# Two composed weights in the setup of a gated recurrent layer, made ahead of the inp product, and the order of the first loads and steps

## The chip, the cores and the metric

The kernel runs on one core of one Trainium2 chip. The metric is the time of one execution on the device in microseconds (us); the changed kernel is compared with this one by the median of their runs. The engines are TensorE (PE), VectorE (DVE), ScalarE (ACT), GpSimd (POOL) and SyncE (SP), which here only issues DMAs. Each runs its own queue of instructions in order and waits on semaphores.

## The reference

x and the context are (32, 128, 256) float32: 32 sequences of 128 steps. For each step, with k = v = context and q = the normalised x:

```
r = decay * r + k * v;  retained = q * r
inp = retained @ Wi.T + bi
gate = sigmoid(inp @ Wg.T + bg)
state = tanh((gate * state + (1 - gate) * inp) @ A.T + inp @ Bm.T)
out = state @ Wo.T + bo
```

Then x = x + tanh(g) * out, a layer norm, and a feed-forward layer: a shared SwiGLU part plus the two best of 8 experts with their softmax weights; it is added to x with a factor tanh(g_ffn).

## The kernel before

The 128 steps are cut into 16 tiles of 8 steps; a tile is 256 tokens (8 steps by 32 sequences). Tile by tile the kernel normalises x, turns the context, squares it, scans it (r), multiplies (ret), splits ret in a high and a low half, and makes three products of ret: inp, gate, and the Bm addend. gate and Bm need products of weights, Wi with Wg and Wi with Bm ("composed" weights), made once in the setup. A recurrence step (L602, L607) adds A times the blended state to the bank rec; ScalarE takes the tanh (`tanh_step`, L1004), and VectorE blends state and gate for the next step (`gated_state`, L1315 u_hi, L1317 u_full, L1320 u_lo). The step that works on tile i also carries parts of tiles i+1, i+2 and of the feed-forward layer of i-1, i-2 between its 8 steps. All these places are written out by hand, one list for each engine; the semaphores setup_pe, setup_dve and setup_act count the setup's results, so each wait names a position in another engine's list.

The setup is one straight list on each engine ahead of the loop, with tile 0's work and its 8 steps in it. `square` loads a 256 x 256 weight, `load_x` and `load_c` load a tile of x (one DMA) and of the context (four DMAs with rows of 32 numbers). On TensorE: WARMUP = 6 products of the identity with itself (L731), Wi, Wg and Bm transposed (L554), tile 0's x transposed (L668), the composed Wg (L562) into bank rec[1], the inp product (L577), 16 small products for the biases (L749), the gate product, A transposed, the composed Bm (L562) into rec[1] again, tile 1's x transposed, Wo transposed (L763), the addends with Bm and with A (L719), and step 0. ScalarE copies each result out of its bank (L1113 to L1131) and squares the context (L1015); VectorE makes the low halves (L1275). Behind step 5 stand the column norms of the weights sh and w1 (L788), whose maxima VectorE takes (L1568), and the scales of the feed-forward weights; ScalarE scales and casts sh and w1 in these steps, and GpSimd makes their low halves (L1840, sh_lo and w_lo).

Of the kernel before, what the change touches and what calls it, by code (L numbers as in the profile page):

```python
# [44 lines left out]
P = 128  # L45
B, S, D = 32, 128, 256
KC = D // P
# [57 lines left out]
def gated_layer(nc, x, ctx_in, g_xattn, g_ffn, Wi, bi, Wg, bg, A, Bm, Wo, bo, decay,  # L105
                w_shared_in, w_shared_out, w1_shared, w2, w_gate, gate_bias, out):
    with ExitStack() as stack:
# [323 lines left out]
        def _(sp):  # L431
# [13 lines left out]
            def square(n, w):  # L445
                sp.dma_start(raw_sq[n][:, :, :], w.rearrange("(k p) i -> p k i", p=P)).then_inc(load[n], 16)

            load_x(0, first)
            square("Wi", Wi)
            square("Wg", Wg)  # L450
            load_c(0, first)
            with nc.allow_non_contiguous_dma(reason="small vectors"):
                square("Bm", Bm)
                load_x(1, first)
                square("A", A)
# [93 lines left out]
        def _(pe):  # L549
# [179 lines left out]
            for n in range(WARMUP):  # L729
                at = slice((n * P) % (KC * TOK), (n * P) % (KC * TOK) + P)  # L730
                pe.matmul(flat(rec[0][:, :, :])[:, at], ident[:, :], ident[:, :], start=(n == 0),  # L731
                          stop=(n == WARMUP - 1), skip_group_check=True)
            pe.wait_ge(load["Wi"], 16)
            transposed(bank[3], raw_sq["Wi"]).then_inc(setup_pe, 1)
            pe.wait_ge(load["Wg"], 16)
# [3 lines left out]
            x_transposed(0, first)  # L739
            pe.wait_ge(setup_act, 3)  # L740
            composed(flat(rec[1][:, :, :]), WgT).then_inc(setup_pe, 1)
            pe.wait_ge(setup_dve, 2)
            inp_product(0, first)
            pe.wait_ge(load["biases"], BIASES)
            pe.wait_ge(setup_act, 4)
# [11 lines left out]
            composed(flat(rec[1][:, :, :]), BmT).then_inc(setup_pe, 1)  # L757
            x_transposed(1, first)
            pe.wait_ge(load["Wo"], 16)
            pe.wait_ge(setup_dve, 6)  # L760
# [5 lines left out]
            pe.wait_ge(setup_act, 6)  # L766
            pe.wait_ge(setup_dve, 7)
            addend_bm(0, first)
            addend_a(0, first)
            pe.wait_ge(setup_dve, 8)  # L770
            recurrence(0, 0, first)
            inp_product(1, first)
            recurrence(0, 1, first)
            gate_product(1, first)
            recurrence(0, 2, first)
# [8 lines left out]
            pe.wait_ge(scale_chain, 1)  # L784
            pe.wait_ge(squares_ready, 2)
            for n, at in (("sh", bank[0]), ("w1", bank[5])):
# [3 lines left out]
                last.then_inc(wsum_done, 1)  # L790
            recurrence(0, 6, first)
            recurrence(0, 7, first)
# [205 lines left out]
        def _(act):  # L998
# [20 lines left out]
            def bias_set(a, k):  # L1019
# [3 lines left out]
                if k.static and a == 0:  # L1023
                    act.wait_ge(setup_dve, 6)
# [86 lines left out]
            context_squares(0, first)  # L1111
# [3 lines left out]
            act.copy(flat(WgT[:, :, :]), bank[4][:, :]).then_inc(setup_act, 1)  # L1115
            act.wait_ge(setup_pe, 3)
# [886 lines left out]
```

## Time and profile before

| | us |
|---|---|
| median of 3 runs (lowest, highest) | 480.12 (478.55, 481.08) |
| the profiled execution's own time | 479.74 |
| its span | 478.0 |
| TensorE busy in the span | 424.7 |
| VectorE busy | 359.7 |
| ScalarE busy | 224.3 |
| GpSimd busy | 194.4 |

A timeline row has the start in us from the span's start, the time in us it covers, the engine (PEld is TensorE's weight load, SPq the issuing queue), the line, operation, what it writes <- reads, and how many instructions; in brackets how long the engine idled before it and what ended that. A float32 product shows as two matmuls in the rows of the same count. "Granted clock" is the clock of TensorE as a share of its full 2.4 GHz; the lower level is 1.2 GHz.

### The profile page before, as it was taken

The numbers are of one execution on the slowest core, as the hardware profiler recorded it, in microseconds if no ns is written. First come the engines' busy times: TensorE is split into PE (matmuls) and PEld (weight loads), VectorE is DVE, ScalarE is ACT, GpSimd is POOL, SyncE is SP. The second block draws the span as 40 slices with busy tenths as digits, with TensorE's granted clock in tenths as the row PEclk, the third lists the DMA queues.
The fourth block names the chain that finished last, engine by engine and source line by source line (L and its number), as shares of the span: only waits on it lengthen the run. The fifth ranks groups of instructions, "written<-read, shape, count | busy, mean of one in ns | idle before, by whom it ended". The sixth has DMA issues, their size and how long they took to land.

```text
span 478.0 us, 12307 instructions
## 1 busy us (share of the span) xinstructions
PE 424.7 (89%) x4348; PEld 355.9 (74%) x4348; DVE 359.7 (75%) x1305; ACT 224.3 (47%) x526; POOL 194.4 (41%) x231
## 2 busy tenths in 40 slices
PE   5987699998988989999989889998997979999890
PEld 4974588787877878988778779887986856865650
DVE  2687979898998777758897777779776675566785
ACT  3564456676746354636464546363643331331300
POOL 3011302442437530202275665432676551447641
PEclk9999889999999999999999999999998988999996
DMA  6786050505243453753441179793236675599862
GB/s 158 203 242 159 2 154 3 143 22 136 45 135 87 147 113 82 162 112 99 102 112 57 45 138 226 169 168 122 100 111 131 169 144 130 166 216 219 207 239 105
DMA packets 110283, 63.08 MB, mean 132 GB/s; under 512 B 80400, under 2 KB 100240, under 8 KB 110224
## 3 DMA queue, kind: packets, MB, share of 16 engines
q1 hardware_dynamic: 105104, 48.66, 42.2%
q0 software_dynamic: 5120, 13.64, 10.4%
q8 instruction: 36, 0.59, 0.5%
q14 instruction: 23, 0.19, 0.1%
HBM read 24.26 MB, written 27.53 MB: 108 GB/s over the span
## 4 chain that ended last, share of the span: by engine, by line
PE 51%; DVE 26%; issue 8%; ACT 3%; DMA 3%; POOL 3%; DVEq 0%; POOLq 0%; ACTq 0%
PE bank L577 11%; PE bank L588 10%; PE bank L635 10%; PE rec L719 5%; PE rec L602 4%; DVE u_hi L1315 4%; DVE r L1424 2%; PE rec L607 2%; DVE u_full L1317 2%; PE bank L867 2%; PE rec L577 2%; ACT state L1004 2%; DVE hs L1650 1%; DVE ret L1437 1%; PE rec L588 1%
## 5 line engine op out<-in xcount | busy, mean ns | idle before, releaser
L1004 ACT ACTIVATE state<-rec 128x64 f32<-128x64 f32 x128 | 36.6, 286 | 156.3 <-PE rec L607 156.2
L1315 DVE SCALAR_TENSOR_TENSOR u_hi<-gt,state 128x64 f16<-128x64 f32 x127 | 39.2, 309 | 68.7 <-ACT state L1004 68.5
L1897 POOL DMA_INDIRECT hrows<-hid_rows,slots_i x52 | 58.5, 1124 | 72.9 <-ACT state L1004 34.4
L1910 POOL DMA_INDIRECT yg<-yrows,slots_i x52 | 53.6, 1032 | 40.4 <-ACT state L1004 18.4
L602 PE MATMUL rec<-u_hi,a_hi 128*128 128x32 f16 x512 | 48.3, 196 | 15.8 <-DVE u_hi L1315 15.7
L602 PEld LDWEIGHTS rec<-u_hi,a_hi 128*128 128x128 f16 x512 | 37.0, 99 | 23.9 <-DVE u_hi L1315 20.3
L602 PE MATMUL rec<-u_hi,a_lo 128*128 128x32 f16 x512 | 47.7, 194 | 0.0
L1840 POOL TENSOR_TENSOR hs_lo<-hs,hs_hi 128x512 f16<-128x512 f32 x14 | 16.2, 1157 | 56.0 <-ACT hs_hi L1205 56.0
L607 PE MATMUL rec<-u_lo,a_hi 128*128 128x32 f16 x512 | 36.5, 195 | 1.0
L602 PEld LDWEIGHTS rec<-u_hi,a_lo 128*128 128x128 f16 x512 | 35.5, 99 | 1.9 <-issue 0.9
L1317 DVE SCALAR_TENSOR_TENSOR u_full<-gt,state 128x64 f32<-128x64 f32 x127 | 35.8, 282 | 0.0
L577 PE MATMUL bank<-xn_hi,sh_hi 128*128 128x256 f16 x128 | 34.9, 273 | 0.0
L577 PE MATMUL bank<-xn_lo,sh_hi 128*128 128x256 f16 x128 | 34.9, 273 | 0.0
L577 PE MATMUL bank<-xn_hi,sh_lo 128*128 128x256 f16 x128 | 34.9, 273 | 0.0
L635 PE MATMUL bank<-w_hi,raw_w 128*128 x144 | 28.7, 286 | 5.4 <-issue 2.9
L867 PE MATMUL bank<-whole_wo,state 128*128 128x256 f32 x128 | 33.0, 403 | 0.0
L1847 POOL TENSOR_TENSOR rs<-ve,minus_half 128x2 f32<-128x2 f32 x16 | 12.3, 769 | 49.8 <-DVE nm L1492 49.8
L1320 DVE TENSOR_TENSOR u_lo<-u_full,u_hi 128x64 f16<-128x64 f32 x127 | 28.8, 226 | 4.4
L719 PE MATMUL rec<-cn,whole_a 128*128 128x256 f32 x128 | 31.4, 388 | 0.2 <-DVE cn L1458 0.2
L588 PE MATMUL bank<-w_hi,xn_hi 128*128 128x256 f16 x104 | 28.5, 274 | 3.0 <-DVE hs L1650 2.9
L588 PE MATMUL bank<-w_lo,xn_hi 128*128 128x256 f16 x104 | 28.4, 273 | 0.0
L588 PE MATMUL bank<-w_hi,xn_lo 128*128 128x256 f16 x104 | 28.4, 273 | 0.0
(299 smaller groups left out, 1390.9 us busy)
## 6 DMA issues: line engine op xcount, KB each, us to landing
yrows<-squares_w SPq DMA_DIRECT2D x20, 256.0 KB
yrows<-squares_sh SPq DMA_DIRECT2D x18, 256.0 KB, 3.0
x_sb<-in_x_dram SPq DMA_DIRECT2D x16, 256.0 KB, 3.4
c_sb<-in_ctx_dram SPq DMA_DIRECT2D x64, 64.0 KB
xr_sb<-in_x_dram SPq DMA_DIRECT2D x16, 256.0 KB, 3.9
hrows<-zeros SPq DMA_DIRECT2D x4, 1024.0 KB, 5.9
raw_w<-in_L_ffn_w_dram SPq DMA_DIRECT2D x8, 256.0 KB, 5.0
out_dram<-raw_w SPq DMA_DIRECT2D x8, 256.0 KB, 2.5
```

The costliest lines, as they stand in the source:

```text
L577: last = pe.matmul(o, w[:, kc, at], a[:, kc, :], start=first, stop=(kc == KC - 1 and w is w_lo), skip_group_check=True)
L588: last = pe.matmul(dst, a[:, kc, s * P:(s + 1) * P], w(part, kc), start=first, stop=(kc == KC - 1 and a is a_lo), skip_group_check=True)
L602: pe.matmul(o[:, oc, :], w[:, kc, oc * P:(oc + 1) * P], u_hi[t % 2][:, kc, :], start=False, stop=False, skip_group_check=True)
L607: last = pe.matmul(o[:, oc, :], a16[0][:, kc, oc * P:(oc + 1) * P], u_lo[t % 2][:, kc, :], start=False, stop=(kc == KC - 1), skip_group_ch ...
L635: last = pe.matmul(dst[:, b * D:(b + 1) * D], hid_t[n % RING][:, half * KC + kc, b * P:(b + 1) * P], split["w2"][part][:, kc, bass.ds(e, 1 ...
L719: last = pe.matmul(rec[a % 2][:, oc, :], whole_a[:, kc, oc * P:(oc + 1) * P], cn[a % 2][:, kc, :], start=False, stop=(kc == KC - 1), skip_ ...
L867: last = pe.matmul(bank[B_WO][:, s * D:(s + 1) * D], state[c % 2][:, kc, s * P:(s + 1) * P], whole_wo[:, kc, :], start=False, stop=(kc == ...
L1004: act.activation(step_of(state[i % 2], t), step_of(rec[i % 2], t), ACT.Tanh, scale=1.0 / PSCALE).then_inc(st_ready, 1)
L1315: dve.scalar_tensor_tensor(out=u_hi[p][:, :, :], in0=gate, scalar=1.0, in1=old, op0=ALU.add, op1=ALU.mult).then_inc(uh_ready, 1)
L1317: dve.scalar_tensor_tensor(out=u_full[p][:, :, :], in0=gate, scalar=1.0, in1=old, op0=ALU.add, op1=ALU.mult).then_inc(uf_ready, 1)
L1897: pool.indirect_dma_start(hrows[q % 2], bass.IndirectOffsetOnAxis(ap=slots_i[q][:, at:at + 1], axis=0), hid_rows[t % 6][:, s, :, :].rearra ...
L1910: pool.indirect_dma_start(yg[t % FETCHED][:, s, pick, :], None, yrows[q % 2][0:blocks_of(q) * P, :], bass.IndirectOffsetOnAxis(ap=slots_i[ ...
```

## The change

SyncE issues tile 0's context ahead of Wg, and A ahead of tile 1's x. TensorE gets six more products of the identity behind Wi's transpositions, then tile 0's x, then Wg and Bm; both composed weights follow at once, Wg's in rec[1], Bm's in rec[0]. The Bm addend, the A addend and step 0 come right behind A's transpositions, and tile 1's and Wo's transpositions behind step 0; tile 1's inp product comes behind step 1 and its gate product behind step 2, and one of the two column norms behind step 6. ScalarE copies WgT before it squares tile 0's context, copies the composed Bm before the inp bias, and normalises x of tile 1 behind it. VectorE makes inp_lo before it turns the context, bm_lo right behind gate_lo, blends for step 1 before tile 1's ret, blends tile 1's input (`blend`) behind step 3's blend and takes the second norm maximum behind the blend of step 8. The numbers in the waits follow.

```diff
@@ -447,12 +447,12 @@
...
     square("Wi", Wi)
+    load_c(0, first)
     square("Wg", Wg)
-    load_c(0, first)
     with nc.allow_non_contiguous_dma(reason="small vectors"):
         square("Bm", Bm)
+        square("A", A)
         load_x(1, first)
-        square("A", A)
         load_c(1, first)
...
@@ -726,23 +726,29 @@
...
     pe.wait_ge(consts, 1)
-    for n in range(WARMUP):
-        at = slice((n * P) % (KC * TOK), (n * P) % (KC * TOK) + P)
-        pe.matmul(flat(rec[0][:, :, :])[:, at], ident[:, :], ident[:, :], start=(n == 0),
-                  stop=(n == WARMUP - 1), skip_group_check=True)
+    def kept_busy(products):
+
+        for n in range(products):
+            at = slice((n * P) % (KC * TOK), (n * P) % (KC * TOK) + P)
+            pe.matmul(flat(rec[0][:, :, :])[:, at], ident[:, :], ident[:, :], start=(n == 0),
+                      stop=(n == products - 1), skip_group_check=True)
+
+    kept_busy(WARMUP)
     pe.wait_ge(load["Wi"], 16)
     transposed(bank[3], raw_sq["Wi"]).then_inc(setup_pe, 1)
+    kept_busy(6)
+    x_transposed(0, first)
     pe.wait_ge(load["Wg"], 16)
...
     transposed(bank[5], raw_sq["Bm"]).then_inc(setup_pe, 1)
-    x_transposed(0, first)
     pe.wait_ge(setup_act, 3)
     composed(flat(rec[1][:, :, :]), WgT).then_inc(setup_pe, 1)
+    pe.wait_ge(setup_act, 4)
+    composed(flat(rec[0][:, :, :]), BmT).then_inc(setup_pe, 1)
     pe.wait_ge(setup_dve, 2)
...
     pe.wait_ge(load["biases"], BIASES)
-    pe.wait_ge(setup_act, 4)
     for n, m in enumerate((WgT, BmT)):
...
@@ -754,25 +760,23 @@
...
     transposed(bank[5], raw_sq["A"]).then_inc(setup_pe, 1)
-    composed(flat(rec[1][:, :, :]), BmT).then_inc(setup_pe, 1)
+    pe.wait_ge(setup_dve, 4)
+    addend_bm(0, first)
+    pe.wait_ge(setup_act, 7)
+    addend_a(0, first)
+    pe.wait_ge(setup_dve, 8)
+    recurrence(0, 0, first)
     x_transposed(1, first)
     pe.wait_ge(load["Wo"], 16)
-    pe.wait_ge(setup_dve, 6)
     for kr in range(KC):
...
     last.then_inc(setup_pe, 1)
-    pe.wait_ge(setup_act, 6)
-    pe.wait_ge(setup_dve, 7)
-    addend_bm(0, first)
-    addend_a(0, first)
-    pe.wait_ge(setup_dve, 8)
-    recurrence(0, 0, first)
+    recurrence(0, 1, first)
     inp_product(1, first)
-    recurrence(0, 1, first)
+    recurrence(0, 2, first)
     gate_product(1, first)
-    recurrence(0, 2, first)
     recurrence(0, 3, first)
...
@@ -781,14 +785,19 @@
...
     addend_a(1, first)
-    pe.wait_ge(scale_chain, 1)
-    pe.wait_ge(squares_ready, 2)
-    for n, at in (("sh", bank[0]), ("w1", bank[5])):
+
+    def column_norms(n, at):
+
...
+
+    pe.wait_ge(scale_chain, 1)
+    pe.wait_ge(squares_ready, 2)
+    column_norms("sh", bank[0])
     recurrence(0, 6, first)
+    column_norms("w1", bank[5])
     recurrence(0, 7, first)
...
@@ -1108,44 +1117,44 @@
...
     x_normalised(0, first)
-    context_squares(0, first)
     act.wait_ge(setup_pe, 1)
...
     act.copy(flat(WgT[:, :, :]), bank[4][:, :]).then_inc(setup_act, 1)
+    context_squares(0, first)
     act.wait_ge(setup_pe, 3)
...
     act.copy(flat(split["gate"][0][:, :, :]), flat(rec[1][:, :, :])).then_inc(setup_act, 1)
-    x_normalised(1, first)
+    act.wait_ge(setup_pe, 5)
+    act.copy(flat(split["bm"][0][:, :, :]), flat(rec[0][:, :, :])).then_inc(setup_act, 1)
     act.wait_ge(load["biases"], BIASES)
     inp_biased(0, first)
+    x_normalised(1, first)
     bias_set(0, first)
-    act.wait_ge(setup_dve, 5)
+    act.wait_ge(setup_dve, 6)
     gate_tanh(0, first)
-    act.wait_ge(setup_pe, 6)
+    act.wait_ge(setup_pe, 7)
     act.mul(flat(whole_a[:, :, :]), bank[5][:, :], -0.5 * PSCALE).then_inc(setup_act, 1)
     act.mul(flat(a16[0][:, :, :]), bank[5][:, :], 0.5 * PSCALE).then_inc(setup_act, 1)
-    act.wait_ge(setup_pe, 7)
-    act.copy(flat(split["bm"][0][:, :, :]), flat(rec[1][:, :, :])).then_inc(setup_act, 1)
     context_squares(1, first)
     bias_set(1, first)
-    ret_high(1, first)
     act.wait_ge(load["small"], SMALL)
...
     tanh_step(0, 0, first)
+    ret_high(1, first)
     act.wait_ge(load["sh"], 16)
...
     tanh_step(0, 1, first)
-    inp_biased(1, first)
     act.wait_ge(load["w1"], 16)
...
     tanh_step(0, 2, first)
+    inp_biased(1, first)
+    tanh_step(0, 3, first)
     gate_tanh(1, first)
-    tanh_step(0, 3, first)
     x_normalised(2, first)
...
@@ -1504,37 +1513,38 @@
...
     first_moments(0)
+    dve.wait_ge(setup_act, 2)
+    low(flat(split["inp"][1][:, :, :]), bank[3][:, :], flat(split["inp"][0][:, :, :]), setup_dve)
     context_turned(0, first)
...
     last.then_inc(setup_dve, 1)
-    dve.wait_ge(setup_dve, 1)
+    dve.wait_ge(setup_dve, 2)
     scanned(0, first)
     retained(0, first)
-    dve.wait_ge(setup_act, 2)
-    low(flat(split["inp"][1][:, :, :]), bank[3][:, :], flat(split["inp"][0][:, :, :]), setup_dve)
     ret_low(0, first)
...
     low(flat(split["gate"][1][:, :, :]), flat(rec[1][:, :, :]), flat(split["gate"][0][:, :, :]), setup_dve)
+    dve.wait_ge(setup_act, 6)
+    low(flat(split["bm"][1][:, :, :]), flat(rec[0][:, :, :]), flat(split["bm"][0][:, :, :]), setup_dve)
     dve.wait_ge(load["biases"], BIASES)
-    dve.wait_ge(setup_pe, 5)
+    dve.wait_ge(setup_pe, 6)
     dve.tensor_tensor(half_gate_bias[:, :], bank[4][:, 0:KC], cols[:, KC:2 * KC], ALU.add).then_inc(setup_dve, 1)
-    dve.wait_ge(setup_dve, 4)
+    dve.wait_ge(setup_dve, 5)
     dve.tensor_scalar(half_gate_bias[:, :], half_gate_bias[:, :], 0.5, None, ALU.mult).then_inc(setup_dve, 1)
...
     dve.wait_ge(setup_act, 8)
-    low(flat(split["bm"][1][:, :, :]), flat(rec[1][:, :, :]), flat(split["bm"][0][:, :, :]), setup_dve)
     dve.scalar_tensor_tensor(out=flat(a16[1][:, :, :]), in0=bank[5][:, :], scalar=0.5 * PSCALE,
...
     scanned(1, first)
+    gated_state(0, 0, first)
     retained(1, first)
     ret_low(1, first)
-    gated_state(0, 0, first)
     dve.wait_ge(setup_act, 9)
...
@@ -1548,9 +1558,9 @@
...
     context_turned(2, first)
-    blend(1, first)
     weight_max("sh", SH, 16)
     gated_state(0, 3, first)
+    blend(1, first)
     weight_max("w1", W1, 16)
...
@@ -1563,10 +1573,14 @@
...
     gated_state(0, 6, first)
-    for n, at in enumerate((bank[0], bank[5])):
+    def largest_norms(n, at):
+
...
+
+    largest_norms(0, bank[0])
     gated_state(0, 7, first)
+    largest_norms(1, bank[5])
     dve.wait_ge(scale_chain, 9)
...
```

## Rows read from the trace of the kernel before

**Rows 1.** The page: busy us, share and instructions; the chain that ended last.

```profile
PE 424.7 (89%) x4348; PEld 355.9 (74%) x4348; DVE 359.7 (75%) x1305; ACT 224.3 (47%) x526; POOL 194.4 (41%) x231
...
PE 51%; DVE 26%; issue 8%; ACT 3%; DMA 3%; POOL 3%; DVEq 0%; POOLq 0%; ACTq 0%
```

**Rows 2.** A stretch: length, busy PE, PEld, DVE, ACT, POOL, granted clock, DMA share, GB/s.

```profile
100.00:200.00 100.00, 92.91 (x1057) 81.34 (x1057) 83.13 (x319) 59.09 (x142) 39.78 (x47) 1.00 0.42 105
```

**Rows 3.** Timeline of SyncE's queue, first 9 us; last, a DMA row ending in us to landing.

```profile
2.16 0.48 SPq L446 DMA_DIRECT2D raw_Wg<-in_L_xattn_Wg_dram  x1
...
2.68 2.31 SPq L443 DMA_DIRECT2D c_sb<-in_ctx_dram  x4
...
5.03 2.87 SPq L446 DMA_DIRECT2D raw_Bm<-in_L_xattn_Bm_dram  x1
...
8.56 0.59 SPq L446 DMA_DIRECT2D raw_A<-in_L_xattn_A_dram  x1
...
raw_A<-in_L_xattn_A_dram SPq DMA_DIRECT2D x1, 256.0 KB, 4.2
```

**Rows 4.** Timeline of TensorE, the setup and the steps 0, 7 and 8.

```profile
1.63 2.93 PE L731 MATMUL rec<-ident 128*128 128x128 f32 x12 [1.63 <-POOL ident L1836]
...
4.76 1.11 PE L554 MATMUL bank<-ident,raw_Wi 128*128 128x128 f32 x4 [0.20 <-DMA raw_Wi<-in_L_xattn_Wi_dram]
...
8.54 1.11 PE L554 MATMUL bank<-ident,raw_Wg 128*128 128x128 f32 x4 [2.67 <-DMA raw_Wg<-in_L_xattn_Wg_dram]
...
10.96 1.12 PE L554 MATMUL bank<-ident,raw_Bm 128*128 128x128 f32 x4 [1.30 <-DMA raw_Bm<-in_L_xattn_Bm_dram]
...
12.72 3.67 PE L562 MATMUL rec<-WgT,raw_Wi 128*128 128x256 f32 x8
...
15.83 0.76 PE L577 MATMUL bank<-ret_hi,inp_hi 128*128 128x256 f32 x1
...
21.39 1.89 PE L562 MATMUL rec<-BmT,raw_Wi 128*128 128x256 f32 x8
...
24.73 0.36 PE L577 MATMUL rec<-ret_hi,bm_hi 128*128 128x256 f32 x1
...
27.97 0.19 PE L602 MATMUL rec<-u_hi,a_hi 128*128 128x32 f16 x1
...
46.50 0.20 PE L602 MATMUL rec<-u_hi,a_hi 128*128 128x32 f16 x1 [1.42 <-DVE u_hi L1315]
...
48.31 0.20 PE L602 MATMUL rec<-u_hi,a_hi 128*128 128x32 f16 x1 [1.08 <-DVE u_hi L1315]
```

**Rows 5.** Timeline of ScalarE: context squares, bm_hi and tile 1's ret_hi.

```profile
10.44 1.17 ACT L1015 ACTIVATE c<-c_turned 128x256 f32<-128x256 f32 x2 [2.85 <-DVE c_turned L1417]
...
23.32 0.58 ACT L1131 CAST bm_hi<-rec 128x512 fp32r<-128x512 f32 x1 [0.29 <-PE rec L562]
...
27.43 0.62 ACT L1053 CAST ret_hi<-ret 128x512 fp32r<-128x512 f32 x1 [1.73 <-DVE ret L1437]
```

**Rows 6.** Timeline of VectorE: context, scan, ret_lo and blends.

```profile
9.69 0.71 DVE L1417 STREAM_TRANSPOSE c_turned<-c_sb 128x512 f32<-128x512 f32 x1 [4.31 <-DMA c_sb<-in_ctx_dram]
...
25.25 1.36 DVE L1424 TENSOR_TENSOR_SCAN r<-dmask,c 128x576 f32<-128x576 f32 x1
...
28.09 0.69 DVE L1275 TENSOR_TENSOR ret_lo<-ret,ret_hi 128x512 fp32r<-128x512 f32 x1 [0.68 <-ACT ret_hi L1053]
...
31.31 0.28 DVE L1315 SCALAR_TENSOR_TENSOR u_hi<-gt,state 128x64 f16<-128x64 f32 x1 [0.72 <-ACT state L1004]
...
38.43 0.26 DVE L1315 SCALAR_TENSOR_TENSOR u_hi<-gt,state 128x64 f16<-128x64 f32 x1
...
45.44 1.01 DVE L1315 SCALAR_TENSOR_TENSOR u_hi<-gt,state 128x64 f16<-128x64 f32 x1 [2.56 <-ACT state L1004]
```

**Rows 7.** Timeline of GpSimd, 44 to 47 us.

```profile
44.20 2.12 POOL L1840 TENSOR_TENSOR sh_lo<-raw_sh,sh_hi 128x1024 f16<-128x1024 f32 x1 [8.89 <-ACT sh_hi L1156]
```

**Rows 8.** Chain of waits, in order of time: start, us, engine, tile, line.

```profile
41.30 3.43 PE bank L788 x8
```

More of the change, by code:

```diff
@@ L1023, in bias_set @@
                 if k.static and a == 0:
-                    act.wait_ge(setup_dve, 6)
+                    act.wait_ge(setup_dve, 7)
                 if k.static and a == 1:
```

## The prediction

> **What bounds the kernel now.** Read first the shares of the page: TensorE is busy 89% of the span, VectorE 75%, and the chain that ended last runs over TensorE for 51% and VectorE for 26% [rows 1]. Next the table by stretches: between 100 and 200 us TensorE works 92.91 of 100 us at the full clock (1.00, the 2.4 GHz level) [rows 2]. There the kernel is a loop bound by TensorE, and the change touches nothing in it. So a gain or loss of the setup is carried to the end as a shift of the whole loop, and what matters is by how much the loop's first steps move. That is read from the timelines of single engines over the first 60 us. TensorE gets to the first recurrence step at 27.97 us [rows 4], but look at what follows: VectorE starts the blend for step 2 only at 31.31, after 0.72 of idling, and that for step 5 at 38.43, with no idle bracket on the row [rows 6]. Between these two VectorE has no idle time: it sets the steps, and TensorE waits for it. (Steps are counted through, the first of tile 0 is step 0; tile 1 begins with step 8.) An earlier first step is worth only what VectorE can pass on.
>
> **Loads.** SyncE issues Wg at 2.16, the four context loads in 2.31 us from 2.68, then Bm, whose issue takes 2.87 us from 5.03 behind the contexts' short packets (4 x 64 KB in rows of 32 numbers) [rows 3]. Wg is first used at 8.54, the contexts at 9.69, Bm at 10.96 [rows 4, 6]. Afterwards the contexts are issued 0.52 earlier (the pitch of Wg's issue, 2.68 - 2.16) and share the engines with nothing: I take 9.1 us for them (bounds 8.5 and 9.7). Wg takes the place of Bm, 0.52 earlier: 10.96 - 0.52 = 10.4 us. Bounds: not before the contexts (9.1), and not after A's old landing, 12.8 (its issue at 8.56 plus 4.2 to landing [rows 3]). I keep 10.4 since Bm's row has the same size and the same packets ahead. Bm then comes at about 11.3, under Wg's processing.
>
> One rule speaks against this. The row shows that Wg, issued ahead of the contexts, still needed 6.4 us from issue to use [rows 3, 4], as if the two shared the engines. The Trainium skill (DMA: Bandwidth & Descriptors, "Queues, rings and completion order") says that an engine consumes descriptors in ring order, while one that comes later may finish first. By ring order Wg would trail the whole context and land at 10.4; by sharing, about with the contexts, which would give back up to 0.5 us. The sum does not use this.
>
> **TensorE up to the inp product.** Before, six warm-up products run 1.63 to 4.56, Wi's transpositions 4.76 to 5.87, then it idles to 8.54. The transpositions of Wg and Bm take 1.11 and 1.12 for four, and composing Wg takes 3.67 against 1.89 for the same shape later [rows 4]: the engine was at the 1.2 GHz level until 16.4, where within the inp product a matmul falls from 0.76 to 0.31. It rose after unbroken work from 10.96. Now six more products (2.93 at most) and tile 0's transpositions (four, so 1.1) follow Wi's: busy from 1.63 to about 9.9 with one gap of 0.2 us. That is more unbroken work than the 5.4 us before the old rise, so I take the clock as up by then. Composing both then costs 1.89 each.
> The Trainium skill (TensorE: Matmul & The Clock Gate, "Part 1: The HAM clock gate") says that activity releases the throttle and that the monitor runs on its own time, whatever the kernel does; so two executions need not rise at the same place, and this step is the one I trust least.
>
> **The queue that this lengthens.** ScalarE now copies WgT before it squares tile 0's context. Behind that wait stand the squares, BmT, ret_high; and VectorE's scan. Chain: Wg at 10.4, transposed 11.05 (1.11 by the ratio 1.89 / 3.67 is 0.57, and the way to ScalarE), WgT copied (0.58, the same shape as bm_hi) 11.65, squares (1.17) 12.85, scan (1.36) 14.2, ret (0.8) 15.0, ret_high (0.65) 15.7, ret_low (0.7) 16.4, inp product 16.5 [rows 4 to 6]. Before, the squares started at 10.44, waiting for nothing but the contexts; the inp product began at 15.83 and was slow in its first matmul. Composing Wg (11.75 to 13.65) and Bm (13.65 to 15.55) fits beside that chain: no cost. The products end at about 18.0 instead of 17.7. The bias and gate products keep their lengths, so gate product, gate tanh and blend are 0.3 later: a small loss.
>
> **TensorE from the gate product to step 0.** What goes from here: Bm's composing (1.89), tile 1's and Wo's transpositions, and a small wait: from the start of composing (21.39) to addend_bm's first product (24.73) lie 3.3 us [rows 4]. addend_bm now starts at 21.39 + 0.3 + 0.2 for the end of A's last transposition and ScalarE's preset of the bias = 21.9, and step 0 at 25.2 instead of 27.97: 2.8 earlier. Cover: by the same chain bm_lo ends at about 18.9 and a_lo at 24.3, before they are wanted; if a_lo came later than 25.2, step 0 would come with it.
>
> **How much VectorE passes on.** ScalarE loses bm_hi (0.58 at 23.32, with 0.29 of waiting) between a_hi and tile 1's squares [rows 5], but starts 0.3 late: squares 23.8 becomes 23.55, scan 25.05 for 25.25. VectorE now does the blend for step 1 (0.65) before it multiplies tile 1's ret: ret 27.05, ret_high 27.8, ret_low 28.5 to 29.15, against 28.09 [rows 6]. The inp product of tile 1 therefore starts at 29.2, not earlier than the old ret_low allowed (28.78); the first step's 2.8 us is spent in front of it. Before, the end of ret_low (28.78) and the start of the idle time (31.31 - 0.72 = 30.59) lay 1.8 apart: 0.7 of blend and 1.1 of memsets and maxima. The latter follow ret_low now, and the blend for step 2 starts at 30.25 instead of 31.31. The 0.72 of idling is gone; that is the gain. The work from there to the blend for step 5 is the same 7.12 us (38.43 - 31.31) with no gap, so that one starts at 37.4: 1.0 earlier. The scan of tile 2 no longer waits 0.17 (1.2 earlier at its end), and so the scales, and sh's high half on ScalarE (ends 42.85).
>
> **Where the halves of the column norms help, and what eats it.** TensorE did both norms before step 6, 3.43 us in the chain of waits [rows 8]. Now only one stands there: step 6 at 41.85 instead of 41.30 + 3.43 = 44.7, more than 2.7 earlier. But ScalarE gets to its tanh only at 42.85 (behind sh's cast), and at 42.95 GpSimd starts sh_lo, 2.12 us. In the trace the blend that started inside sh_lo took 1.01 us instead of 0.27 and ended 0.13 after it [rows 6, 7]. So the blend for step 7 stands from 43.2 until 45.07 + 0.13. Step 7 at 45.25 instead of 46.50 (gain 1.25), step 8 at 46.65 instead of 48.31 [rows 4], since only one norm maximum stands before its blend; the second takes 0.3 back at step 9, which leaves 1.3 to 1.4. Bounds of this place: 1.0 (the sum of the scales alone) and 2.7 (no collision). In tile 1's steps VectorE meets w_lo on GpSimd in the same way as before, only earlier. I carry 1.3.
>
> **Sum.** The profiled execution took 479.74 us for a span of 478.0. 479.74 - 1.3 = 478.4. The three timed runs have their median at 480.12, 0.4 above it; as a median I give 480.12 - 1.3 = 478.8.
>
> **Rivals.**
> First, the clock does not rise before composing. For it: 4.04 us of work up to 5.87 did not raise it. Against it: the work is now twice as long. Price: composing Wg 12.3 to 16.0 and Bm to about 18.6 with a rise on the way, inp product 18.6 instead of 16.5, all of it on the path: 2.1. 478.8 + 2.1 = 480.9. It is slower than before; it decides once composing ends 1.3 us later than ret_low, at 17.7.
> Second, Wg lands late. Each microsecond after 10.4 goes straight into the path through ScalarE's wait. At A's old 12.8 it is 2.4: 481.2, slower. It decides from 11.7 on.
> Third, more is passed on than I say: the blend escapes sh_lo, or the whole 2.8 us of step 0 survives, or one stretch at the low clock less occurs later (before steps 7 and 8 TensorE idles 1.42 and 1.08 [rows 4], the kind of place behind which the clock can fall). 480.12 - 2.8 to 3.3 = about 477.0. Against it: the VectorE chain above.
> Fourth, nothing arrives: some other transfer or wait sets the loop's start. 480.1.
>
> **Chances.** Forecast 0.43 (its own range 477.6 to 479.9), clock 0.13, Wg 0.12, more passed on 0.24, nothing 0.08. Within 0.5% (2.4 us) of the median is about what a measurement here cannot tell from no change. Of the third case nearly all is faster than that, with a little of the forecast: 0.27. The first two rivals alone stay within it (480.9, 481.2); slower by more takes both at once (483.3), or Wg later than A's old place, or a loss that I don't see: 0.12. The rest, 0.61, is within. Range 476.0 to 481.6: the two mechanisms of loss and most of the third case are in it.
>
> **What would show it.** Wg's transpositions at 10.4, taking 0.6 and not 1.1; both composings of 1.9; inp product at 16.5; step 0 near 25.2; the inp product of tile 1 still at 29; the blend for step 7 stretched to about 2 us beside sh_lo; step 8 near 46.7. The forecast is wrong if step 0's gain appears whole at step 2, if Wg comes after 11.7, or if composing takes 3.7.

## The result and the profile after

The changed kernel takes 476.59 us, median of 20 runs (471.84 to 479.21), against 480.0 us of the kernel before in 20 runs beside it (476.04 to 482.53). The ratio is 0.9914, with a 95% interval of 0.9886 to 0.9942: 3.4 us faster. The ratio leaves out three slow executions of the changed kernel, over 1.5% above its fastest, so it is a little below the quotient of the two medians. The forecast was 1.3 us and 478.8; its range (476.0 to 481.6) held the time, and faster by over 0.5% had a chance of 0.27. A second measurement on another occasion gave 476.67 against 479.52, ratio 0.9926 (0.9894 to 0.9957); its profiled execution is called the second trace below. The profiled execution took 475.4 us, span 473.7, against 479.74 and 478.0.

The page of the changed kernel, shares and chain. The engines do the same work in a shorter span, and VectorE's share of the chain is 28% now [rows 1]:

```profile
PE 422.1 (89%) x4360; PEld 354.1 (75%) x4360; DVE 360.6 (76%) x1305; ACT 223.9 (47%) x526; POOL 194.1 (41%) x231
PE 48%; DVE 28%; issue 8%; ACT 3%; DMA 3%; POOL 3%; DVEq 0%; POOLq 0%; ACTq 0%
```

SyncE's queue: start, us, what. The contexts are issued at 2.15, Wg at 4.53, and Bm's issue takes 1.70 us where it took 2.87 [rows 3] (the old order of loads has 1.59 and 1.60 in the two other traces with it, so 2.87 was one case of several):

```profile
2.15 2.33 SPq L443 DMA_DIRECT2D c_sb<-in_ctx_dram  x4
4.53 0.63 SPq L446 DMA_DIRECT2D raw_Wg<-in_L_xattn_Wg_dram  x1
5.20 1.70 SPq L446 DMA_DIRECT2D raw_Bm<-in_L_xattn_Bm_dram  x1
```

TensorE's timeline; in brackets the idle time before a row and what ended it. Against [rows 4]:

```profile
9.22 0.66 PE L554 MATMUL bank<-ident,raw_Wg 128*128 128x128 f32 x4 [0.90 <-DMA raw_Wg<-in_L_xattn_Wg_dram]
11.26 0.66 PE L554 MATMUL bank<-ident,raw_Bm 128*128 128x128 f32 x4 [1.38 <-DMA raw_Bm<-in_L_xattn_Bm_dram]
11.75 1.89 PE L562 MATMUL rec<-WgT,raw_Wi 128*128 128x256 f32 x8
13.48 1.89 PE L562 MATMUL rec<-BmT,raw_Wi 128*128 128x256 f32 x8
15.34 0.36 PE L577 MATMUL bank<-ret_hi,inp_hi 128*128 128x256 f32 x1
...
20.52 0.36 PE L577 MATMUL rec<-ret_hi,bm_hi 128*128 128x256 f32 x1
23.91 0.19 PE L602 MATMUL rec<-u_hi,a_hi 128*128 128x32 f16 x1
27.68 0.35 PE L577 MATMUL bank<-ret_hi,inp_hi 128*128 128x256 f32 x1 [1.54 <-DVE ret_lo L1284]
...
43.42 0.20 PE L602 MATMUL rec<-u_hi,a_hi 128*128 128x32 f16 x1 [1.08 <-DVE u_hi L1324]
44.90 0.20 PE L602 MATMUL rec<-u_hi,a_hi 128*128 128x32 f16 x1 [0.75 <-DVE u_hi L1324]
```

Both composings take 1.89 (Wg's took 3.67). Step 0 is at 23.91 instead of 27.97, step 7 at 43.42 instead of 46.50, step 8 at 44.90 instead of 48.31: 4.1, 3.1 and 3.4 earlier. ScalarE in the same stretch: the squares of the context (L1024) start behind the copy of WgT, 0.05 us before the old 10.44, and those of tile 1 at 22.20 [rows 5]:

```profile
9.91 0.58 ACT L1123 COPY WgT<-bank 128x512 f32<-128x512 f32 x1 [1.83 <-PE bank L554]
10.39 1.17 ACT L1024 ACTIVATE c<-c_turned 128x256 f32<-128x256 f32 x2
...
22.20 1.22 ACT L1024 ACTIVATE c<-c_turned 128x256 f32<-128x256 f32 x2
```

VectorE: the blends for steps 1, 2, 5 and 7 (L1324) and ret_low of tile 1; those for steps 2 and 5 were at 31.31 and 38.43 [rows 6]. Below it GpSimd, whose sh_lo was at 44.20 [rows 7]:

```profile
24.78 0.28 DVE L1324 SCALAR_TENSOR_TENSOR u_hi<-gt,state 128x64 f16<-128x64 f32 x1
...
26.84 0.69 DVE L1284 TENSOR_TENSOR ret_lo<-ret,ret_hi 128x512 fp32r<-128x512 f32 x1 [0.68 <-ACT ret_hi L1062]
...
28.48 0.28 DVE L1324 SCALAR_TENSOR_TENSOR u_hi<-gt,state 128x64 f16<-128x64 f32 x1
...
35.61 0.27 DVE L1324 SCALAR_TENSOR_TENSOR u_hi<-gt,state 128x64 f16<-128x64 f32 x1
...
41.24 2.12 DVE L1324 SCALAR_TENSOR_TENSOR u_hi<-gt,state 128x64 f16<-128x64 f32 x1 [1.43 <-ACT state L1013]
```

```profile
41.11 2.13 POOL L1854 TENSOR_TENSOR sh_lo<-raw_sh,sh_hi 128x1024 f16<-128x1024 f32 x1 [8.64 <-ACT sh_hi L1165]
```

Past the setup, the starts of ScalarE's tanh in both traces are the measure: the changed kernel is 3.44 us ahead at step 12 (56.50 for 59.94), 4.5 from step 16 (67.53 for 72.05) to step 116 (356.55 for 361.00), 6.6 at step 120, and 4.3 at the end. The jump behind step 12 is a stretch of low granted clock that the kernel before has and the changed one has not. The next one, 2.1 us between steps 116 and 118, is by 1.5 such a stretch (from TensorE's first product with raw_w, L635, to the tanh of step 118 it takes 3.42 before and 1.90 changed) and by 0.6 a longer wait ahead of these products (2.93 before, 2.31 changed). First the kernel before, then the changed one; columns as in [rows 2], the clock is the third from the end:

```profile
60.00:65.00 5.00, 5.00 (x40) 4.85 (x39) 3.13 (x15) 3.20 (x8) 1.02 (x2) 0.66 0.35 79
367.00:372.00 5.00, 3.88 (x27) 3.16 (x28) 0.17 (x2) 0.46 (x2) 1.31 (x2) 0.66 1.08 262
```

```profile
60.00:65.00 5.00, 4.42 (x40) 3.57 (x38) 4.35 (x12) 3.08 (x8) 0.00 (x0) 1.00 0.81 187
367.00:372.00 5.00, 5.00 (x72) 4.57 (x70) 4.11 (x24) 1.58 (x4) 3.03 (x3) 1.00 1.09 244
446.00:451.00 5.00, 3.32 (x18) 2.54 (x19) 3.09 (x7) 0.55 (x1) 0.00 (x0) 0.66 0.91 273
100.00:200.00 100.00, 92.90 (x1055) 81.32 (x1054) 81.75 (x313) 56.87 (x137) 38.74 (x44) 1.00 0.47 111
```

The row from 100 us is the loop, equal to [rows 2] in TensorE's time. The low stretch between 446 and 451 only the changed kernel has; it gives part of it back. A single execution thus gains or loses 1 to 2 us at such a place; the setup's own part is what stands at step 8. (In the first 16 us of the kernel before the same column shows 1.00, though its shapes take 1.11 for 0.66 and 3.67 for 1.89 there; in the setup the level is therefore read from the durations.)

### The profile page after: what moved, and what is told of

The parts are those of the page before. It is cut to its first block, busy times and chain, and to the rows that moved or that the text cites. A ratio compares the mean times of both kernels' runs of the same rounds, so it can differ in the third digit from the quotient of the medians.

```text
span 473.7 us, 12330 instructions
## 1 busy us (share of the span) xinstructions
PE 422.1 (89%) x4360; PEld 354.1 (75%) x4360; DVE 360.6 (76%) x1305; ACT 223.9 (47%) x526; POOL 194.1 (41%) x231
## 4 chain that ended last, share of the span: by engine, by line
PE 48%; DVE 28%; issue 8%; ACT 3%; DMA 3%; POOL 3%; DVEq 0%; POOLq 0%; ACTq 0%
PE bank L588 10%; PE bank L577 10%; PE bank L635 9%; PE rec L719 5%; DVE u_hi L1324 4%; PE rec L602 4%; DVE r L1433 3%; DVE u_full L1326 2%; PE rec L607 2%; PE bank L876 2%; PE rec L635 2%; DVE ret L1446 2%; DMA raw_sh<-hrows 1%; ACT state L1013 1%; PE rec L588 1%
## 5 line engine op out<-in xcount | busy, mean ns | idle before, releaser
L1324 DVE SCALAR_TENSOR_TENSOR u_hi<-gt,state 128x64 f16<-128x64 f32 x127 | 40.4, 318 | 63.2 <-ACT state L1013 63.1
L635 PE MATMUL bank<-w_hi,raw_w 128*128 x144 | 27.7, 279 | 5.0 <-issue 2.5
L588 PE MATMUL bank<-w_hi,xn_hi 128*128 128x256 f16 x104 | 28.5, 274 | 3.0 <-DVE hs L1664 2.9
```

What stands on the lines that cost most here:

```text
L588: last = pe.matmul(dst, a[:, kc, s * P:(s + 1) * P], w(part, kc), start=first, stop=(kc == KC - 1 and a is a_lo), skip_group_check=True)
L635: last = pe.matmul(dst[:, b * D:(b + 1) * D], hid_t[n % RING][:, half * KC + kc, b * P:(b + 1) * P], split["w2"][part][:, kc, bass.ds(e, 1 ...
L1324: dve.scalar_tensor_tensor(out=u_hi[p][:, :, :], in0=gate, scalar=1.0, in1=old, op0=ALU.add, op1=ALU.mult).then_inc(uh_ready, 1)
```

## The experiments

Each kernel is the changed one with one edit, save the fourth. "Step 8" is the start of its tanh on ScalarE: 49.08 before, 45.67 changed. The time given for the first eight is one execution's, beside one of the kernel before on the same chip (479.07 for the first four, 479.48 for the next four); these scatter by 2 us and more, so the position of the steps decides. Wg is first used at another time in each trace (9.22 in the changed kernel's), and where the queue waits for it, all later steps shift with it; this shift is named where it matters.

**Without the six products.**

```diff
     transposed(bank[3], raw_sq["Wi"]).then_inc(setup_pe, 1)
-    kept_busy(6)
     x_transposed(0, first)
```

> The changed kernel without the six products behind Wi's transpositions. Measure: the start of ScalarE's tanh of step 8, the first of tile 1 (49.08 us before, 45.67 changed), which tells the setup apart from stretches of low clock further on. Theory A: the six products are what lets both composings run at the full clock. Then composing takes 3.7 us and up to 3.7 more, inp product starts near 18 instead of 15.34, step 8's tanh between 47.4 and 48.6. Rival: TensorE has slack there, or the clock rises by itself: step 8 at 45.7 (within 0.3).

Time 478.41; step 8 at 47.25. TensorE's timeline:

```profile
8.67 0.66 PE L554 MATMUL bank<-ident,raw_Wg 128*128 128x128 f32 x4 [0.37 <-DMA raw_Wg<-in_L_xattn_Wg_dram]
10.03 1.12 PE L554 MATMUL bank<-ident,raw_Bm 128*128 128x128 f32 x4 [0.70 <-DMA raw_Bm<-in_L_xattn_Bm_dram]
10.94 3.62 PE L562 MATMUL rec<-WgT,raw_Wi 128*128 128x256 f32 x8
14.35 2.73 PE L562 MATMUL rec<-BmT,raw_Wi 128*128 128x256 f32 x8
```

The clock was up at Wg (0.66 for four) and down again at Bm (1.12). Composing then held up the inp product (16.73 for 15.34), and step 8 came 1.58 later, just under the 47.4 that theory A gives. So in this execution leaving the six products out cost 1.6, though Wg came 0.55 earlier than in the changed kernel's trace; the timed runs below say what they are worth in the median.

**Loads in the old order.**

```diff
     square("Wi", Wi)
-    load_c(0, first)
     square("Wg", Wg)
+    load_c(0, first)
...
         square("Bm", Bm)
-        square("A", A)
         load_x(1, first)
+        square("A", A)
```

> The changed kernel with the loads in the order of before (Wg, contexts, Bm, x of tile 1, A). Theory A: the new order of loads brings nothing, since the squares start when both the context and WgT are there: contexts at 9.7, squares near 10.5 against 10.39; step 8's tanh at 45.5 to 46.0. Rival: the earlier contexts are part of the gain: step 8 at 46.3 or later.

Time 480.42; Wg transposed at 8.13, inp product at 15.17, step 8 at 45.48 (changed: 45.67). The load order brings nothing. The time is not shorter for all that: at step 116 the tanh is at 358.77 where the changed kernel has 356.55. Of these 2.2 us 1.9 arise between steps 12 and 13, behind a stretch at a granted clock of 0.66 (53 to 63 us).

**Wg behind Bm.**

```diff
     load_c(0, first)
-    square("Wg", Wg)
     with nc.allow_non_contiguous_dma(reason="small vectors"):
         square("Bm", Bm)
+        square("Wg", Wg)
```

> The changed kernel with Bm's load ahead of Wg's, so that Wg lands where Bm did (11.26 instead of 9.22). It tests the step of the prediction that each microsecond of Wg's landing goes straight into the path through ScalarE's wait. By it the squares, ret and everything up to step 8 come 2.0 us later: step 8's tanh at 47.4 to 47.9. Rival: VectorE and the collision with sh_lo absorb it as they absorbed the gain: 45.7 to 46.5.

Time 476.16; step 8 at 46.50. Wg came at 10.05, not at the 11.26 that Bm had:

```profile
10.05 0.66 PE L554 MATMUL bank<-ident,raw_Wg 128*128 128x128 f32 x4 [1.77 <-DMA raw_Wg<-in_L_xattn_Wg_dram]
10.54 0.60 PE L554 MATMUL bank<-ident,raw_Bm 128*128 128x128 f32 x4
```

Wg is 0.83 later (10.05 - 9.22) and step 8 is 0.83 later (46.50 - 45.67). The second trace of the changed kernel agrees: Wg 1.06 later (10.28), step 8 1.06 later (46.73). The mechanism of theory A is right, one to one through ScalarE's wait; its size was wrong because the landing was, and 46.50 alone would also have met the rival's upper end.

**The kernel before with the six products alone.**

```diff
     transposed(bank[3], raw_sq["Wi"]).then_inc(setup_pe, 1)
+    for n in range(6):
+        at = slice((n * P) % (KC * TOK), (n * P) % (KC * TOK) + P)
+        pe.matmul(flat(rec[0][:, :, :])[:, at], ident[:, :], ident[:, :], start=(n == 0),
+                  stop=(n == 5), skip_group_check=True)
```

> The kernel before with the six products behind Wi's transpositions alone. Theory A: composing Wg takes 1.9 instead of 3.7, the inp product starts near 15.3 at the full clock and ends 0.9 earlier, and all steps up to step 8 come 0.9 earlier: its tanh at 48.2 instead of 49.08 (0.9 of the 3.4 gained). Rival one: the whole gain of 3.4 is the clock's, 45.7. Rival two: nothing, 49.1, because tile 0's transpositions still stand behind Bm and the clock has fallen again by then.

Time 481.41; step 8 at 48.97. TensorE:

```profile
7.36 0.66 PE L554 MATMUL bank<-ident,raw_Wg 128*128 128x128 f32 x4
10.30 0.66 PE L554 MATMUL bank<-ident,raw_Bm 128*128 128x128 f32 x4 [2.28 <-DMA raw_Bm<-in_L_xattn_Bm_dram]
10.79 0.60 PE L668 MATMUL bank<-ident,xn 128*128 128x128 f32 x4
12.62 3.35 PE L562 MATMUL rec<-WgT,raw_Wi 128*128 128x256 f32 x8 [1.23 <-ACT WgT L1119]
```

The clock was up and fell behind the waits of 2.28 and 1.23; composing took 3.35. The products give nothing by themselves (0.11 at step 8), as the second rival has it.

**Tile 1's and Wo's transpositions back ahead of step 0.**

```diff
     transposed(bank[5], raw_sq["A"]).then_inc(setup_pe, 1)
+    x_transposed(1, first)
+    pe.wait_ge(load["Wo"], 16)
+    for kr in range(KC):
...
+    last.then_inc(setup_pe, 1)
+    pe.wait_ge(setup_dve, 7)
     pe.wait_ge(setup_dve, 4)
     addend_bm(0, first)
...
     recurrence(0, 0, first)
-    x_transposed(1, first)
-    pe.wait_ge(load["Wo"], 16)
-    for kr in range(KC):
...
-    last.then_inc(setup_pe, 1)
```

> The changed kernel with tile 1's and Wo's transpositions back between A's and addend_bm (1.5 us of TensorE ahead of step 0). Theory A: in the changed kernel VectorE's blend for step 1 stands ahead of tile 1's ret and already starts just when its scan ends (24.78), so step 0's delay is passed on whole: step 0's tanh at 26.0, step 8's at 47.1 instead of 45.67. Rival, the prediction's view that step 0's time is spent in front of tile 1's ret anyway: step 8 at 45.7 to 46.0.

Time 479.5; step 8 at 47.09, 1.42 later; step 0's tanh at 25.35 for 24.46, 0.89 later. VectorE's blend for step 1 waits for that tanh, and TensorE's inp product of tile 1 runs partly at the low clock (its first matmul takes 0.55 for 0.35, the others 0.41 for 0.28):

```profile
25.66 0.27 DVE L1325 SCALAR_TENSOR_TENSOR u_hi<-gt,state 128x64 f16<-128x64 f32 x1 [1.00 <-ACT state L1014]
...
28.55 0.55 PE L577 MATMUL bank<-ret_hi,inp_hi 128*128 128x256 f32 x1 [1.84 <-DVE ret_lo L1285]
```

The delay of step 0 is not hidden, as theory A has it: the blends for steps 1 and 2 come 0.88 and 0.87 later. The other 0.5 arises behind the slow inp product, at the blend for step 3 (32.25 for 30.92), and the changed kernel's trace has no such stretch there. So the place of these transpositions is worth 0.9, or 1.1 with Wg at 9.01 here, and that 47.09 meets the expected 47.1 is luck.

**Bm composed behind A's transpositions, as before.**

```diff
     composed(flat(rec[1][:, :, :]), WgT).then_inc(setup_pe, 1)
-    pe.wait_ge(setup_act, 4)
-    composed(flat(rec[0][:, :, :]), BmT).then_inc(setup_pe, 1)
...
     transposed(bank[5], raw_sq["A"]).then_inc(setup_pe, 1)
-    pe.wait_ge(setup_dve, 4)
+    composed(flat(rec[1][:, :, :]), BmT).then_inc(setup_pe, 1)
+    pe.wait_ge(setup_dve, 7)
     addend_bm(0, first)
```

(bm_high goes behind a_high on ScalarE, bm_low behind the blend on VectorE.)

> The changed kernel with Bm's composing back behind A's transpositions (into rec[1], bm_hi and bm_lo behind a_hi and the blend of tile 0, as before). Theory A: step 0 comes 2.3 later (1.9 of composing and the wait for bm_lo), ScalarE's chain to tile 1's squares gets 0.6 longer, and all of the 2.3 reaches step 8: its tanh at 47.8 to 48.2. Rival: only ScalarE's 0.6 to 0.9 is passed on, step 8 at 46.3 to 46.6.

Time 483.74; step 8 at 49.41, 3.74 later. TensorE:

```profile
21.00 1.89 PE L562 MATMUL rec<-BmT,raw_Wi 128*128 128x256 f32 x8
24.30 0.39 PE L577 MATMUL rec<-ret_hi,bm_hi 128*128 128x256 f32 x1 [1.40 <-DVE bm_lo L1284]
```

The Bm addend goes from 20.52 to 24.30, 3.78 later: 1.89 of composing, 1.40 of waiting for bm_low, and 0.49 of Wg's landing (9.71 for 9.22). The place of this one product is worth 3.2 us at step 8 (3.74 less the 0.49), 1.0 more than expected, and nearly as much as the whole change. The parts don't add up, since each is taken back with the others in place.

**Both column norms together ahead of step 6.**

```diff
     column_norms("sh", bank[0])
-    recurrence(0, 6, first)
     column_norms("w1", bank[5])
+    recurrence(0, 6, first)
```

> The changed kernel with both column norms ahead of step 6. Theory A: the blend for step 7 ends with GpSimd's sh_lo (43.4) in either case, so step 6 comes 1.7 later (tanh near 42.7 instead of 40.94) and step 8 not at all: 45.5 to 45.9. Rival: the split is worth its 1.7 us: step 8 at 47.3.

Time 476.22; step 6 at 42.45, 1.51 later, but step 8 at 45.82, 0.15 later. VectorE's blend for step 7:

```profile
42.77 0.75 DVE L1324 SCALAR_TENSOR_TENSOR u_hi<-gt,state 128x64 f16<-128x64 f32 x1 [2.80 <-ACT state L1013]
```

It ends 0.13 after sh_lo (41.27, 2.12 long here), as the changed kernel's 2.12 us blend ends 0.12 after its own. Wg was in use at 9.36 in this trace, 0.14 later, which is all but 0.01 of the 0.15. What the split of the norms gives is spent inside that collision.

**The low halves of sh and w1 on VectorE.**

```diff
+    dve.wait_ge(wide_hi, 1)
+    low(flat(split["sh"][1][:, :, :]), flat(raw_wide["sh"][:, :, :]), flat(split["sh"][0][:, :, :]), wide_lo)
...
+                if i == 1:
+                    dve.wait_ge(wide_hi, 3)
+                    low(flat(split["w1"][1][:, :, :]), flat(raw_wide["w1"][:, :, :]), flat(split["w1"][0][:, :, :]), wide_lo)
...
-    pool.wait_ge(wide_hi, 1)
-    low(flat(split["sh"][1][:, :, :]), flat(raw_wide["sh"][:, :, :]), flat(split["sh"][0][:, :, :]), wide_lo)
...
-    pool.wait_ge(wide_hi, 3)
-    low(flat(split["w1"][1][:, :, :]), flat(raw_wide["w1"][:, :, :]), flat(split["w1"][0][:, :, :]), wide_lo)
```

> The changed kernel with both low halves, sh_lo and w_lo, made by VectorE (two float32 inputs of 1,024 columns, 1.3 us each by the 0.69 of 512 columns): sh_lo behind the blend for step 7, w_lo ahead of the blend for step 13. Theory A: the blend for step 7 and the variance of tile 3, which each last 2.1 us beside GpSimd, last 0.3; step 8's tanh at 44.6 to 45.0 instead of 45.67, step 12's at 53.8 to 55.0 instead of 56.50. Rival: what VectorE no longer waits it now works, and nothing moves (45.7 and 56.5) or it gets later.

Time 471.6; step 8 at 44.31 (1.36 earlier), step 12 at 53.16 (3.34 earlier). Wg came 0.41 earlier (8.81), so the edit itself gives 0.95 and 2.9. VectorE: the blend for step 7, and the two low halves:

```profile
40.83 0.28 DVE L1324 SCALAR_TENSOR_TENSOR u_hi<-gt,state 128x64 f16<-128x64 f32 x1 [1.43 <-ACT state L1013]
...
41.49 1.22 DVE L1284 TENSOR_TENSOR sh_lo<-raw_sh,sh_hi 128x1024 f16<-128x1024 f32 x1
...
54.66 1.22 DVE L1284 TENSOR_TENSOR w_lo<-raw_w,w_hi 128x1024 f16<-128x1024 f32 x1
```

VectorE does in 1.22 us what GpSimd needs 2.13 for, and does it in a place of its own choosing.

**Timed runs.** Four kernels, 6 or 12 executions each, against 479.52 (23 executions) of the kernel before:

> The changed kernel, timed against the one before in five rounds, and as the base of the other three. Its setup gains 3.4 us at step 8; stretches of low clock further on scatter each execution by a few us. Ratio 0.990 to 0.996.

> The changed kernel with both low halves on VectorE, timed. One look gave 3.3 us at step 12 over the changed kernel. If that shift is kept to the end as the trace shows, the ratio to before is 0.983 to 0.989 (about 472 us), 3 us better than the changed kernel. Rival: the one look was a lucky order of the clock's stretches, ratio as the changed kernel's.

> The changed kernel without the six products, timed. In one look the clock was up at tile 0's transpositions, fell before Bm's and composing took 3.6 and 2.7; step 8 came 1.6 later. If that is the rule, it is 1.0 to 2.5 us slower than the changed kernel; the rival, that the six products matter in no more than a few executions, gives less than 0.7.

> The changed kernel with Bm's composing back behind A's transpositions, timed. One look had step 8 at 49.4 against 45.67 (3.7 later, of which 0.5 was the contexts' and Wg's landing in that execution). By theory A the place of this one step is worth nearly the whole gain: ratio to before 0.997 to 1.004. Rival: the look was unlucky, ratio 0.994 or less.

| kernel | median us (runs) | ratio to before, 95% | Wg used | step 8 | step 12 |
|---|---|---|---|---|---|
| changed, again | 476.67 (12) | 0.9926 (0.9894 to 0.9957) | 10.28 | 46.73 | 57.80 |
| low halves on VectorE | 471.03 (6) | 0.9846 (0.9805 to 0.9886) | 8.73 | 44.24 | 53.41 |
| without the six products | 476.25 (12) | 0.9941 (0.991 to 0.9972) | 8.80 | 45.50 | 56.45 |
| Bm composed late | 484.4 (6) | 1.0124 (1.0077 to 1.0171) | 8.99 | 48.69 | 60.14 |

Low halves on VectorE is the best version: 5.6 us under the changed kernel by the medians, 0.8% by the two ratios (3.8 us), and the intervals don't touch. Its trace is 4.4 us ahead of the second trace at step 12, of which 1.55 is Wg's use at 8.73 for 10.28; so 2.8 us is the edit's, near the 2.9 above, and the rest of the medians' difference is not traced to a place.

The six products, worth 1.6 us in one trace, are not seen in the medians; with 12 executions each a difference below about 2 us would not be. In the second trace without them composing Wg took 2.93 and Bm 1.89, ended at 15.1, and the inp product still began at 15.18.

With Bm composed late the kernel is 4.9 us slower than before, ratio 1.0124 where 0.997 to 1.004 was expected. At step 8 it stands 0.4 ahead of before and at step 12 0.2 behind; against the changed kernel step 8 is 3.02 later with Wg 0.23 earlier, so the place costs 3.2 again. The other 4.5 of the 7.7 us against the changed kernel lie behind the setup, and part of this stands in the two traces of this kernel, which are 0.7 ahead of and level with before at step 116 (360.34 and 361.03 for 361.00) and 1.1 and 1.6 behind it at step 118. TensorE's first product with raw_w between these steps, in the kernel before, in this kernel's trace of the timed runs and in its earlier one:

```profile
368.12 0.39 PE L635 MATMUL bank<-w_hi,raw_w 128*128 x1 [2.93 <-issue]
...
369.38 0.39 PE L635 MATMUL bank<-w_hi,raw_w 128*128 x1 [4.86 <-issue]
...
369.69 0.39 PE L635 MATMUL bank<-w_hi,raw_w 128*128 x1 [4.48 <-issue]
```

The profile names no releaser, but the kernel has TensorE wait there for the transposing load into raw_w (L487). SyncE, which waits for the rows that GpSimd scatters (hrows), issues it 3.6 and 3.4 us after the tanh of step 116, and 1.7 after it in the kernel before. GpSimd issues the scatter 0.85 before that tanh in all three. Of the 14 traces here 4 have the load late (3.1 to 3.6 us; the other two are the six products alone and the transpositions ahead of step 0) and 10 have it at 1.3 to 1.8. Whether late Bm makes this likelier, two traces don't show. The earlier trace (483.74) loses 2.4 us more against before behind the last step, and where the executions without a profile lose is not known: the cause of the whole stays open.

The second trace of the changed kernel is the best check of the forecast, since Wg came where it was expected:

```profile
10.28 0.66 PE L554 MATMUL bank<-ident,raw_Wg 128*128 128x128 f32 x4 [1.84 <-DMA raw_Wg<-in_L_xattn_Wg_dram]
...
16.41 0.35 PE L577 MATMUL bank<-ret_hi,inp_hi 128*128 128x256 f32 x1 [1.08 <-DVE ret_lo L1284]
```

## Why the prediction was wrong in its size

The chain of steps held; three of its terms were mis-sized, all towards too small a gain: Wg's landing (10.4 forecast, 9.22 measured, 1.16 of the error), the chain to tile 1's ret_low (0.6) and what was to be given back behind step 8 (0.4). In the order of the prediction:

**Loads: the step that failed.** Forecast 10.4 for Wg, measured 9.22. Ten traces with the contexts and then Wg at the head of the queue have 8.67 to 10.28, median 9.0. I took Bm's landing of before, less its earlier issue, as Wg's; but that row was one landing out of a wide scatter: the two other traces with the old order of loads have Bm in use at 10.30 and 10.04, not 10.96. From its issue Wg needed 4.7 us (4.53 to 9.22), Bm in the kernel before 5.9 (5.03 to 10.96). The prediction read the rule of ring order (the Trainium skill, DMA: Bandwidth & Descriptors, "Queues, rings and completion order") as Wg landing behind the whole context. The context is in use at 8.72 without a wait, so its landing is not seen; where both are waited for they are in use at 9.68 and 10.28 (second trace) and at 9.19 and 9.71 (Bm composed late), half a microsecond apart, which fits either reading.

**TensorE up to the inp product: right in the number, not in the reason.** 1.89 each, clock up. But the rise needed no six products: in the two traces without them tile 0's transpositions take 0.66 too, and what those kernels then lose is the level, not the rise. The price of the first rival was too high in the median: without the six products it is the same within the intervals. The inp product starts 0.15 behind the end of ret_low in every trace of the changed order but the one with composing at 3.62, also where composing Wg took 2.93. The slack is small, though: in the changed kernel's trace TensorE transposed Bm only at 11.26, ahead of composing, and by the pitch of the two composings (11.75 to 13.48) the second was through at 15.21, 0.13 before the inp product.

**The queue that this lengthens: right in kind.** Squares behind WgT: 11.65 forecast, 10.39 measured, 1.26 earlier, of which Wg's landing is 1.18. Inp product 16.5 forecast, 15.34 measured, 16.41 where Wg came at 10.28. It ends at 16.8 instead of 17.7: 0.9 of gain where I had 0.3 of loss. The experiment with Wg behind Bm and the second trace show that this term is passed on one to one.

**TensorE from the gate product to step 0: right.** Forecast 2.8 from 3.3 removed; from the Bm addend to step 0 it is 3.39 (20.52 to 23.91), forecast 3.3 (21.9 to 25.2). Step 0 is 1.3 earlier than forecast, the inp product's 1.16 carried on.

**How much VectorE passes on: too little by 0.6.** The blend for step 2 was to start at 30.25; it started at 28.48, 1.77 earlier. Of it 1.16 is the inp product's, and 0.6 arose in ScalarE's and VectorE's chain to it (tile 1's ret_low: forecast 28.5, measured 26.84). Nearly 0.4 of this is in the forecast's own sum. In the kernel before ScalarE has

```profile
23.80 0.31 ACT L1013 COPY c<-r 128x64 f32<-128x64 f32 x1
24.01 1.21 ACT L1015 ACTIVATE c<-c_turned 128x256 f32<-128x256 f32 x2
```

so the 23.8 taken for tile 1's squares is the copy ahead of them. And 23.8 less bm_hi's 0.58 and its wait of 0.29, plus the 0.3 of the late start, is 23.2, not 23.55: the wait was named and not taken off. With the squares 0.21 behind and the scan 1.25 behind these, as measured (22.20 and 23.45), that is 24.7 for the scan where the forecast has 25.05. The other 0.2 is in small differences up to the blend for step 2.

Of the 4.06 us gained at step 0 VectorE passed on 2.83 at the blend for step 2, so the loss in front of it was real. That VectorE then sets the steps without a gap was right: from the blend for step 2 to that for step 5 it is 7.13 us (28.48 to 35.61), forecast 7.12.

**Where the halves of the column norms help, and what eats it: right.** Blend for step 7 beside sh_lo: forecast 43.2, 2.0 long; measured 41.24, 2.12 long. Putting the norms together again costs nothing at step 8 once Wg's landing is taken off. The blend starts 0.13 behind sh_lo and ends 0.12 behind its end (43.36 and 43.24), and with sh_lo moved to VectorE it takes 0.28. This agrees with the Trainium skill (SBUF — State Buffer, "SBUF: two separate sides"), by which the port pair that VectorE and GpSimd share is an exclusive lock. The 0.36 that was to be given back behind step 8 came only in part: the gain is 3.41 at step 8, 3.20 at step 9 and 3.44 at step 12, and in the second trace 2.35, 2.15 and 2.14.

**The sum** at step 12: 1.3 forecast, 3.44 measured. The difference of 2.14 is 1.16 from the inp product on (Wg's landing), 0.6 in the chain to tile 1's ret_low, and 0.4 that did not go back. The second trace, with Wg at 10.28, has 2.35 at step 8 and 2.14 at step 12: with the first term nearly as forecast, the others still make it 0.8 more than 1.3. Of the rivals the third (477.0) came nearest in time, but by another way: the blend did not escape sh_lo. "One stretch at the low clock less" was in its text, and the profiled execution has two less and one more; whether the medians owe anything to that is open, since the setup's 3.4 alone is their whole difference.

## What to carry to other kernels

A product that is wanted last in a setup but whose inputs are there first belongs ahead of the work that waits for something else: composing Bm while VectorE and ScalarE prepared ret cost nothing, and where it stood before it cost 3.2 us at the first step, 1.40 of it a wait for its low half that the composing's own row doesn't show. When a forecast rests on the landing of one load, take the range of the landing and not the row, and carry it through the chain one to one if the queue waits for it. Where a blend is stretched beside a GpSimd operation, look at what the blocked engine would need for that operation itself: here moving two of them there gave 2.8 to 2.9 us at step 12, nearly as much as the whole change. And before a step is credited to an edit, take off what the loads did in that execution.

## What the runs showed of the hardware

- The same order of loads had Wg in use between 8.67 and 10.28 us, in ten executions of kernels that are the same up to there but for the warm-up, 4.1 to 6.0 us after its issue. With Wg ahead of the contexts it was in use at 7.36, 8.13 and 8.54, the first two with no wait for it, so it had landed by then.
- VectorE does a 128x1024 subtraction from fp32 to fp16 in 1.22 us, GpSimd in 2.13, and while GpSimd does it VectorE's blend, which reads two tiles, stands still: 2.12 us for an operation of 0.27.
- TensorE's granted clock fell again from the 2.4 to the 1.2 GHz level within the setup after it had risen: behind waits of 2.28 and 1.23 us with little work between them (the kernel before with six products), and behind waits of 1.64, 0.37 and 0.70 in the changed kernel without them (0.66 for Wg's four transpositions, 1.12 for Bm's). The place of such stretches later in the run differs between executions and moves single times by 1 to 2 us each.
- A transposing load of scattered rows was issued 1.3 to 1.8 us after the tanh of step 116 in ten traces and 3.1 to 3.6 us after it in four, with the scatter issued 0.84 to 1.14 before that tanh in all. TensorE idled 1.8 to 2.9 us ahead of the products that read it in the ten, and 4.1 to 4.9 in the four.
